# The first chunk of x in four transfers, its rounded and remainder parts made straight from PSUM, and its plain copy last

## What is computed

```python
xn = _layernorm(x, axis=-1)
# mamba: 512 -> 2 x 1024, split into x and gate; then a convolution of four taps over time and silu
proj = jnp.einsum('bld,ed->ble', hidden_states, in_proj_w)
x, gate = jnp.split(proj, 2, axis=-1)
...
ssm = jnp.einsum('bld,ed->ble', xt, x_proj_w)
...
# experts: 64, of which 6 for each token, up to 64 tokens each, and a shared one
logits = x @ gate_w.T
scores = jax.nn.softmax(logits, axis=-1)
topk_w, topk_i = jax.lax.top_k(scores, K)
```

## Time and profile before

| | us |
|---|---|
| time, median of 3 runs | 1363.42 |
| lowest and highest of them | 1358.88, 1363.46 |
| span of the profiled execution | 1386.3 |
| TensorE busy in it | 1291.9 (93%) |
| VectorE busy | 1095.9 (79%) |
| ScalarE busy | 910.5 (66%) |
| GpSimd busy | 878.1 (63%) |

### The profile page before, as it was taken

One profiled execution on the slowest core, in us unless ns is written; L12 is line 12 of the kernel. 1 busy time (PEld: TensorE's weight loads), 2 busy tenths in 40 slices (PEclk: granted clock), 3 DMA queues, 4 the chain that ended last, 5 costly groups with the idle time before them and its releaser, 6 DMA issues.

```text
span 1386.3 us, 53429 instructions
## 1 busy us (share of the span) xinstructions
PE 1291.9 (93%) x21591; PEld 808.3 (58%) x21591; DVE 1095.9 (79%) x1257; ACT 910.5 (66%) x1914; POOL 878.1 (63%) x522
## 2 busy tenths in 40 slices
PE   4999989699999999999999999999999899999998
PEld 3767767445555545555555555545554577787876
DVE  4798989878988889888888898888898655646554
ACT  3756567478788788887887888777777343434343
POOL 2455448268888988988889889889898421303030
PEclk9999999789999999999999999999999999999999
DMA  8153534859898998998989989989889761313130
GB/s 289 65 224 118 218 120 172 272 170 297 257 295 274 283 269 257 304 280 248 306 259 279 288 248 308 285 252 290 263 255 300 243 231 51 132 45 137 37 144 30
DMA packets 129710, 304.82 MB, mean 220 GB/s; under 512 B 18512, under 2 KB 20304, under 8 KB 127824
## 3 DMA queue, kind: packets, MB, share of 16 engines
q1 hardware_dynamic: 122048, 285.13, 63.3%
q0 software_dynamic: 7600, 18.91, 6.0%
HBM read 213.91 MB, written 56.77 MB: 195 GB/s over the span
## 4 chain that ended last, share of the span: by engine, by line
PE 61%; DVE 11%; issue 6%; DVEq 1%; DMA 1%; ACT 0%; POOL 0%; ACTq 0%; POOLq 0%
PE p_dBx L1313 18%; PE p_y L1322 9%; DVE state L1002 8%; PE p_dBx L1372 7%; PE p_g L1299 6%; PE p_g L1282 6%; PE p_dt L1262 2%; PE p_y L1383 2%; PE p_g L1383 2%; PE p_u L1383 2%; PE p_dt L1383 2%; PE p_u L1268 2%; DVE out_operand_parts L1037 2%; PE p_u L1289 1%; PE p_u L1282 1%
## 5 line engine op out<-in xcount | busy, mean ns | idle before, releaser
L1002 DVE TENSOR_TENSOR_SCAN state<-dA,state_carry,p_dBx 128x512 f32<-128x512 f32 x512 | 626.9, 1266 | 104.3 <-PE p_dBx L1313 96.8
L937 POOL TENSOR_TENSOR h_times_C<-state,C_bcast 128x1024 f32<-128x1024 f32 x128 | 307.1, 2400 | 87.4 <-DVE state L1002 86.6
L1313 PE MATMUL p_dBx<-B_diagonals,step_rows 64*32 64x128 f32 x16384 | 327.9, 275 | 30.0 <-issue 20.4
L1313 PEld LDWEIGHTS p_dBx<-B_diagonals,step_rows 64*32 64x32 f32 x16384 | 242.3, 106 | 178.8 <-issue 176.8
L937 POOL TENSOR_TENSOR C_bcast<-state,C_bcast 128x1024 f32<-128x1024 f32 x128 | 319.9, 2787 | 18.1 <-DVE state L1002 18.1
L1152 ACT ACTIVATE dA<-dt_blocks_odd,A_par 128x512 f32<-128x512 f32 x256 | 169.7, 710 | 14.8 <-DMA dt_blocks_odd<-step_rows 14.8
L1152 ACT ACTIVATE dA<-dt_blocks_even,A_par 128x512 f32<-128x512 f32 x256 | 169.7, 710 | 4.2 <-DMA dt_blocks_even<-step_rows 4.2
L276 POOL TENSOR_TENSOR w_in_parts_lo<-C_bcast,w_in_parts_hi 128x512 fp32r<-128x512 f32 x64 | 89.8, 1406 | 113.0 <-ACT w_in_parts_hi L485 112.8
L952 POOL TENSOR_TENSOR step_rows<-step_rows 128x512 f32<-128x512 f32 x16 | 21.9, 1401 | 182.3 <-DMA step_rows<-moe 182.3
L364 DVE SCALAR_TENSOR_TENSOR conv_out<-conv_in,conv_w,conv_out 128x512 f32<-128x512 f32 x96 | 100.4, 1055 | 10.3 <-ACT conv_out L499 8.0
L1299 PE MATMUL p_g<-w_down_pair,step_rows 128*64 128x512 f32 (+1 forms) x396 | 92.3, 601 | 0.0
(11 more groups left out here) (184 smaller groups left out, 2111.1 us busy)
## 6 DMA issues: line engine op xcount, KB each, us to landing
w_gate_pair<-in_w_gate SPq DMA_DIRECT2D x32, 1408.0 KB
w_up_pair<-in_w_up SPq DMA_DIRECT2D x32, 1408.0 KB, 8.0
w_down_pair<-in_w_down SPq DMA_DIRECT2D x66, 512.0 KB
dt_blocks_odd<-step_rows SPq DMA_DIRECT2D x256, 64.0 KB
dt_blocks_even<-step_rows SPq DMA_DIRECT2D x240, 64.0 KB
w_down_pair<-in_w_down SPq DMA_DIRECT2D x33, 384.0 KB
g_d<-y_gated SPq DMA_DIRECT2D x33, 256.0 KB, 4.8
sz_d<-silu_gate SPq DMA_DIRECT2D x32, 256.0 KB, 2.0
```

The source lines that it names most:

```text
L937: pool.tensor_tensor(hc[m][:, b, :, :], hb[:, q, :, :], Cb[:, NM * cp + GS * m:NM * cp + GS * m + GS, :], ALU.mult).then_inc(s_hc, 1)
L1002: ins = dve.tensor_tensor_scan(hb[:, g % NBUF, s, :], dA[:, g % NBUF, s, :], pB[:, g % 2, :].rearrange("p (t s) -> p s t", s=GS)[:, s, :], ...
L1313: ins = pe.matmul(out[DB * p:DB * p + DB, half, j, :, :], dtxT[k, j * P + DB * b:j * P + DB * b + DB], diag[k, ND * cp + 2 * j + p // 2, a ...
```

## The change

- x of chunk 0 comes in four transfers, one for each token tile, each with a semaphore (`s_x0`); a statistic waits for its own. `s_x` now counts chunks 1 to 3, and chunk 1's load waits for nothing.
- The first part of in_proj's weights is issued directly behind them, ahead of the small weights.
- The small weights are waited for later: on ScalarE behind `take_xT(0)`, on VectorE behind the remainders, on TensorE behind `in_proj(0, 0)`.
- GpSimd sets `mhalf` behind the identity.
- `take_xT(0)` first makes the rounded part, bank by bank (`s_x0hi`); VectorE subtracts it bank by bank straight from PSUM (`s_x0lo`); ScalarE's plain copy follows bank by bank, each behind the subtract of that bank.
- `in_proj(0, 0)` waits bank by bank for the part that a matmul reads. `turn_x(1)`, which writes the banks again, waits for the plain copy and the subtracts of chunk 0.

```diff
--- before.py
+++ after.py
@@ -131,6 +131,8 @@
         pL_scatter = pIn[1][:, 0:NP]
 
         s_x, s_w = sem("x_loaded"), sem("weights_loaded")
+        s_x0hi, s_x0lo = sem("first_x_hi_ready"), sem("first_x_lo_ready")
+        s_x0 = [sem(f"x_first_loaded{j}") for j in range(TJ)]
         s_const, s_ident = sem("constants_set"), sem("identity_set")
         s_var, s_rstd, s_xn = sem("var_ready"), sem("rstd_ready"), sem("xn_ready")
         s_xT, s_xnT = sem("xT_in_psum"), sem("xnT_ready")
@@ -165,16 +167,18 @@
         @block.sync
         def _(sp):
             def load_x(c):
-                if c > 0:
-                    sp.wait_ge(s_x, 16 * c)
+                if c > 1:
+                    sp.wait_ge(s_x, 16 * c - 16)
                 sp.dma_start(x[:, TJ * c:TJ * c + TJ, :], io["x"][c * CH:(c + 1) * CH, :].rearrange("(j p) h -> p j h", p=P)).then_inc(s_x, 16)
 
-            load_x(0)
+            for j in range(TJ):
+                sp.dma_start(x[:, j, :], io["x"][j * P:(j + 1) * P, :]).then_inc(s_x0[j], 16)
+            sp.dma_start(win[:, w_cut[0]:w_cut[1], :], io["w_in"][:, w_cut[0]:w_cut[1], :]).then_inc(s_win[0], 16)
             sp.dma_start(wgate[:, :, :], io["w_router"]).then_inc(s_w, 16)
             sp.dma_start(wxp[:, :, :], io["w_x_proj"]).then_inc(s_w, 16)
             sp.dma_start(cw[:, :, :], io["conv_w"]).then_inc(s_w, 16)
             sp.dma_start(cb[:, :], io["conv_b"]).then_inc(s_w, 16)
-            for n in range(3):
+            for n in range(1, 3):
                 sp.dma_start(win[:, w_cut[n]:w_cut[n + 1], :], io["w_in"][:, w_cut[n]:w_cut[n + 1], :]).then_inc(s_win[n], 16)
             for c in range(1, NCH):
                 load_x(c)
@@ -253,10 +257,10 @@
         def _(pool):
             pool.memset(zero[:, :], 0.0).then_inc(s_z, 1)
             pool.memset(ident[:, :], 0.0).then_inc(s_ident, 1)
-            pool.memset(mhalf[:, :], -0.5).then_inc(s_const, 1)
             pool.wait_ge(s_ident, 1)
             pool.affine_select(out=ident[:, :], in_=ident[:, :], compare_op=ALU.not_equal, fill=1.0, base=0,
                                pattern=[[-1, P]], channel_multiplier=1).then_inc(s_ident, 1)
+            pool.memset(mhalf[:, :], -0.5).then_inc(s_const, 1)
             pool.iota(eioi[:, :, :], [[0, TJ], [1, E]], base=0, channel_multiplier=0).then_inc(s_const, 1)
             pool.iota(tioi[:, :], [[-P, NCH * TJ]], base=T, channel_multiplier=-1).then_inc(s_const, 1)
             pool.iota(sioi[:, :], [[1, CAP]], base=0, channel_multiplier=0).then_inc(s_const, 1)
@@ -337,8 +341,11 @@
 
             def ln_stats(c):
 
-                dve.wait_ge(s_x, 16 * c + 16)
+                if c > 0:
+                    dve.wait_ge(s_x, 16 * c)
                 for j in range(TJ):
+                    if c == 0:
+                        dve.wait_ge(s_x0[j], 16)
                     chain(dve.bn_stats(stats[:, j, :], x[:, c * TJ + j, :]))
                 settled()
                 for j in range(TJ):
@@ -419,8 +426,11 @@
             settled()
             ln_stats(0)
             ln_norm(0)
-            dve.wait_ge(s_xhi, 1)
-            dve.tensor_tensor(xp[1][:, 0, :, :], xnT[:, :, :], xp[0][:, 0, :, :], ALU.subtract).then_inc(s_xlo, 1)
+            for k in range(KH):
+                dve.wait_ge(s_x0hi, k + 1)
+                dve.tensor_tensor(xp[1][:, 0, k, :], pT[:, k, :], xp[0][:, 0, k, :], ALU.subtract).then_inc(s_x0lo, 1)
+            dve.sem_inc(s_xlo, 1)
+            dve.wait_ge(s_w, 64)
             for c in range(NCH):
                 last = c == NCH - 1
                 if c > 0:
@@ -471,8 +481,6 @@
 
         @block.scalar
         def _(act):
-            act.wait_ge(s_w, 64)
-
             def w_hi(c, n):
 
                 c, n = (c, n) if n < 2 * ND else (c + 1, n - 2 * ND)
@@ -487,8 +495,16 @@
             def take_xT(c):
 
                 act.wait_ge(s_xT, c + 1)
-                if c > 0:
-                    act.wait_ge(s_xTs, 16 * c)
+                if c == 0:
+                    for k in range(KH):
+                        act.activation(xp[0][:, 0, k, :], pT[:, k, :], ACT.Copy).then_inc(s_x0hi, 1)
+                    act.sem_inc(s_xhi, 1)
+                    for k in range(KH):
+                        act.wait_ge(s_x0lo, k + 1)
+                        ins = act.activation(xnT[:, k, :], pT[:, k, :], ACT.Copy)
+                    ins.then_inc(s_xnT, 1)
+                    return
+                act.wait_ge(s_xTs, 16 * c)
                 act.activation(xnT[:, :, :], pT[:, :, :], ACT.Copy).then_inc(s_xnT, 1)
                 act.activation(xp[0][:, c % 2, :, :], pT[:, :, :], ACT.Copy).then_inc(s_xhi, 1)
 
@@ -536,6 +552,7 @@
             w_hi(0, 0)
             w_hi(0, 1)
             take_xT(0)
+            act.wait_ge(s_w, 64)
             for c in range(NCH):
                 act.wait_ge(s_conv, ND * c + ND)
                 act.activation(xr[:, :, 0:TAPS - 1], xr[:, :, CH:CH + TAPS - 1], ACT.Copy).then_inc(s_halo, 1)
@@ -593,6 +610,9 @@
             def turn_x(c):
                 if c > 0:
                     pe.wait_ge(s_xhi, c)
+                if c == 1:
+                    pe.wait_ge(s_xnT, 1)
+                    pe.wait_ge(s_x0lo, KH)
                 if c > 1:
                     pe.wait_ge(s_bt, c - 1)
                 for j in range(TJ):
@@ -619,6 +639,8 @@
                 pe.wait_ge(s_wlo, 2 * ND * c + (n + 1))
                 parts = [(p, q, k) for p, q in ((1, 0), (0, 1), (0, 0)) for k in range(KH)]
                 for at, (p, q, k) in enumerate(parts):
+                    if c == 0 and n == 0 and at < 2 * KH:
+                        pe.wait_ge(s_x0lo if q else s_x0hi, k + 1)
                     ins = pe.matmul(pIn[n % 2][:, :], wp[p][:, n % 2, k * P:(k + 1) * P], xp[q][:, c % 2, k, :],
                                     start=at == 0, stop=at == len(parts) - 1)
                 ins.then_inc(s_in if half == "x" else s_zps, 1)
@@ -652,11 +674,13 @@
                 ins.then_inc(s_vps, 1)
 
             turn_x(0)
-            pe.wait_ge(s_w, 64)
             for c in range(NCH):
-                pe.wait_ge(s_xlo, c + 1)
+                if c > 0:
+                    pe.wait_ge(s_xlo, c + 1)
                 in_proj(c, 0)
                 pe.wait_ge(s_xnT, c + 1)
+                if c == 0:
+                    pe.wait_ge(s_w, 64)
                 if c > 0:
                     pe.wait_ge(s_ssm, c)
                 token_halves(c, wgate, xnT, KH, None, s_lps)
```

## The result

The changed kernel took 1357.26 us (median of 20 runs, 1352.07 to 1361.62), the kernel before 1364.15 in the same comparison (20 runs, 1358.88 to 1373.82): ratio 0.9944, 95% interval 0.9927 to 0.9961. That is 5 to 10 us less. In two later comparisons of the same two kernels the ratio was 0.9950 (0.9932 to 0.9967) and 0.9959 (0.9942 to 0.9976).

The account below looks back on a forecast made before the run. No single bound: a dependent chain before 26 us, then VectorE in the first stage. Transfers 1.8 plus transposes to tile's end 5.4 made 7.2 us, taking 1363.4 to 1356.2 us; range 1352.0 to 1361.5.

Parts of the forecast that it names:

- Rival (c): Behind 26 us, some wait on the wall clock eats the head's gain: 1363.4 us; chance 0.06.
- (d): Rival: at the turn of the stages TensorE's low clock lasts longer, 1366 us at 20 us longer; chance 0.04.
- Four transfers, 1.8: Head, x's landing: the fourth quarter lands where the megabyte did, only its own statistic behind it; 1.8 us saved.
- The bounds (0.3 to 2.1): Limits on the transfers' saving: 0.3 us if issue cost delays the fourth, some 2.1 by VectorE's pitch.
- near 4.4: Sign in the profile after: four statistics starting some 0.65 us apart from about 4.4, the last near 6.4.
- The order behind it, 0: Head, weight loads: issuing w_in's first part before the small weights gives nothing by itself, later waits being hidden.
- The slack of 0.5 us: Head: w_in's first remainder ready at 13.5, ahead of the first matmul at 14.0, with w_in landing as before.
- T to the first matmul, 6.11 to 0.73: Head, from the transposes' end (T) to the first in_proj matmul: bank-by-bank rounded copies cut 6.11 us to 0.73.
- The tile as long as before: First in_proj tile: takes the 4.31 us of before, VectorE's remainders not late, ending at T + 5.04.
- Rival (b): First tile onward: TensorE's low clock lasts longer, saving only 1.9 to 4.4 us, 1359.0 to 1361.5; chance 0.08.
- The lists 7 us earlier: Sign: the first convolution and the turn of the stages (270) both come 7 us earlier.
- rival (a): Head: fourth transfer lands late, by 1.5 us (1357.7, chance 0.11) or 3 us (1359.2, chance 0.03).

Follow-up runs that it names:

- the delay: Changed kernel with 26 chained VectorE memsets between chunk 0's landing and its statistics, computing nothing; 1404.46 against the changed kernel's 1382.97 us, ratio 1.0108.
- one transfer: Changed kernel with chunk 0 of x again in a single transfer, the rest as changed; ratio 0.9954 to the kernel before.
- the weights' order as before: Changed kernel with w_in's first part issued behind the small weights and ScalarE's wait for the small weights at the front again; timed once, 1359.7 us.
- the transfers alone: Kernel before with only chunk 0's four transfers and their four semaphores added; ratio 0.9993 to the kernel before.
- the matmuls ahead: Changed kernel with 22 identity matmuls, their result overwritten, ahead of the first transpose; ratio 0.9960 to the kernel before.
- last kernel: Changed kernel with 22 identity matmuls ahead, GpSimd's w_in remainders behind the fourth normalising, and the first tile's rounded parts first; 1352.98 us, 0.9916 of before.

## Why the prediction was right

**The bound and the place.** Right: one chain in the head, VectorE's stage behind it, and the delay shows that the head is passed on whole. Rival (c), a wait on the wall clock, is refuted by it. The granted clock at the turn is 0.50 as in the earlier trace rows; nothing of (d) was seen in the times.

**The sum.** Forecast 7.2 us and a median of 1356.2; measured 1357.26. The heads differ by 31.41 (mean of two profiles) less 25.17 (mean of three), 6.2 us, and the times by 6.9, 7.5 and 5.8. The mechanism was right. Of the 1.0 us that the sum was too large, 0.4 lies in the term of the transfers and 0.4 in a cost that the sum put at nothing.

- *Four transfers, 1.8.* The statistics end 8.92 less 7.48, 1.4 us earlier on average. The fourth quarter did not always land where the megabyte did: over all kernels its statistic started between 6.46 and 7.47, the first statistic of one transfer between 6.41 and 6.48. The bounds (0.3 to 2.1) held; that bytes alone decide did not. The first statistic started at 3.68, not near 4.4, and the four did not follow at VectorE's pace. In the changed kernel's windows packets went at 242 GB/s from 3.5 to 4 us and at 229 from 4 to 5, where before it was 406 from 3.5 to 4. w_in's part right behind them doesn't explain it: with the weights' order as before the fourth statistic started at 7.16. The cause stays open.
- *The order behind it, 0.* This is the step that failed, at its size of 0.4 us. I looked only for what comes too late. With w_in's first part early and ScalarE's table load moved from 10.14 to 0.74, GpSimd's remainders moved onto the third and fourth normalising: 0.65 us in two of three profiles, and none with the weights' order as before. The slack of 0.5 us that I gave the old order was also gone: behind four transfers w_in landed about 1 us later than before (ScalarE's table load, which waits for it, came at 11.04 and 11.21 in the two kernels with the old order, 10.14 before). At T the gain was therefore 15.15 less 14.15, 1.0 us, for the 1.8 and 0 of the sum.
- *T to the first matmul, 6.11 to 0.73.* Measured 0.77 or 0.78 in every profile with the banks. The subtract took 0.68 where 0.71 was taken, and four took 2.48 and not 2.84; the rounded copies stood 0.49 apart, and the plain copy ended at 17.46, 1.75 ahead of its reader.
- *The tile as long as before.* 3.81 to 5.06 us against 4.24 and 4.87. On average the same (4.64 and 4.56), but it is no constant: the rise to the full level came between some 2.7 and 5.4 us behind the first matmul, and in the changed kernel's third profile ahead of it. That the averages agree is partly luck: without that profile the changed kernel's tile is 0.5 us longer. Rival (b) is in that spread, up to 1 us, and did not reach token_halves, which took 1.95 us in every profile but that of the transfers alone (2.07).
- *The lists 7 us earlier.* 269.07 less 261.81 is 7.26, which looks like the sum to the tenth. It is 6.27 of head and 1.0 of clock, as the profile of before had a stretch at 0.97. One pair of profiles would have confirmed a sum that was 1 us too large. The median of the times, 6.9 us, is near the forecast by luck in the same way: three comparisons scatter from 5.8 to 7.5.

The Trainium skill's rule on batching (DMA: Bandwidth & Descriptors, Bandwidth) asks for transfers of 1 MiB or more. Read as fixed parts paid one after another, the 3 us of rival (a), it did not come out: the transfers alone gained 1.7 at T, so the fixed parts overlap. What the Trainium skill tells of frequent short idles (TensorE: Matmul & The Clock Gate, A second HAM failure mode), by which rival (b) had the low level go on through the next tile, did not come out either: here the second tile ran at 0.26 us a matmul or less in every profile. Idle time ahead of the tile may count: with the matmuls ahead TensorE fell back to the low level about a gap of 0.87 us between transposes, with 1.33 us of idle time shortly before.

What stays open: why the granted clock falls in some executions of stage one, which moves a run by 1 to 5 us, as much as the change; how the executions with a short tile differ from those with a long one; why the last quarter of x lands up to 1 us late; and what the waits moved behind, and mhalf set later, give by themselves, which no run tests.

## What to carry to other kernels

When a dependent chain heads a program, hand its tiles on bank by bank in the order in which the reader wants them, and move the copy that nobody waits for to the end. When an edit makes something ready earlier, ask which engine now runs beside whom: a step that was harmlessly late may land on the critical engine's work. And compare profiles at a landmark close to the edit, of more than one execution, before believing a match further down.

## What the runs showed of the hardware

- A VectorE normalising of 128x512 took 0.55 us alone and 1.5 us beside a GpSimd subtract from SBUF (12.16 to 13.69 in the profile of before); its four subtracts out of PSUM took 2.48 us beside one (last kernel) and without.
- A VectorE subtract of 2048 columns took 2.29 us with its first operand in PSUM and in SBUF alike; in four pieces 2.48.
- Sixteen transposes from a standing TensorE stood 0.21 us apart to the last, 3.65 us in all where the normalising did not hold them up. In one of the changed kernel's three profiles the first matmul behind them was at the full level all the same, in two it was not. Right behind matmuls of the identity, issued from 2 us on, the sixteen took 2.02 us.
- ScalarE's first table load came at 0.74 us in every kernel without the wait for the small weights at the front of its program. With that wait it came at 10.14 to 11.21, and the wait that ended just before it was for w_in, not for the small weights, the last of which had landed at 7.8 in the profile of before.
- The same kernel was 1.9% slower on one chip than on the others, and most of the second stage's steps took 24.9 us there, 23.9 to 24.0 on the others.
